# Second layer's combine: three gathered places a tile instead of one running sum

## The chip, the cores and the metric

The kernel runs on one core of one Trainium2 chip. The metric is the device time of one execution in microseconds (us), median of several runs. Engines are called by their names in the profile: PE (TensorE), PEld (its weight loads), DVE (VectorE), ACT (ScalarE), POOL (GpSimd), SP (SyncE, which here only issues DMAs). A queue name such as SPq or POOLq is the part of an engine that issues.

## The reference, cut to what matters

Two layers, each a cross-attention and a mixture-of-experts feed-forward part, work on 2048 tokens of 256 values:

```
x = x + tanh(g_xattn[0]) * L0_xattn(layernorm(x), ctx)
x = x + tanh(g_ffn[0])   * L0_ffn(layernorm(x))      # 8 experts, top 2
x = x + tanh(g_xattn[1]) * L1_xattn(layernorm(x), ctx)
x = x + tanh(g_ffn[1])   * L1_ffn(layernorm(x))      # 16 experts, top 4
return x
# L1_ffn, for the tokens x [2048, 256]:
w_dense = top-4 softmax weights of x @ router_w.T       # [2048, 16]
moe_out = sum over experts e of w_dense[:, e] * (silu(x @ gate_w[e].T) * (x @ up_w[e].T)) @ down_w[e].T
shared  = silu(x @ shared_gate_w.T) * (x @ shared_up_w.T) @ shared_down_w.T
return moe_out + sigmoid(x @ se_gate_w.T) * shared
```

The change is in how the four expert results of a token (moe_out) are brought together in the last line of the kernel's work.

## The kernel before, in words

The 2048 tokens are 16 tiles of 128 (NT = 16), and x_sb holds all of them in on-chip memory (SBUF). In the feed-forward part of the second layer the tokens of each expert are collected into slots of 128 rows. There are 80 such slots in 40 groups (NG[1] = 40), each group with two slots. For a group, POOL gathers token rows (L664), PE multiplies by gate, up and down weights, DVE copies the result to yb (L960), and SP stores it to the table ys[1] in HBM (L649). The tokens' weights are already multiplied in, so a token's expert sum is the plain sum of four rows of ys[1].

The place table says where these four rows are: `place[:, k, t]` holds, for place k of tile t, the row number in ys[1]. Places are in falling order of slot, so place 3 belongs to the lowest expert of a token and place 0 to the highest.

After the last token gather POOL runs `gather_sums(pl, n)` for n = 0 to 3 (L702 to L711). Each n goes over all 16 tiles with place 3 - n. For n = 0 the indirect DMA writes into y_sum[t]; for n = 1 to 3 it adds in memory (`compute_op=ALU.add`). y_sum[t] is one piece of 128x256 f32 a tile, in three old buffers (stg, wqp, xnf). So 16 gathers write and 48 add. Before each n, `needed_rows` (L680) waits until the groups that the n-th expert from the end can reach have been stored; it reads two registers and issues two tiny POOL instructions (L687). From n = 1 on, every second tile waits until the gathers before it on the same two tiles have landed (`sum_ld`, one semaphore for two tiles).

DVE meanwhile works through the shared expert. Its 24 units (NSH = 24: 4 blocks of 512 tokens, 6 units each) are done partly before the expert groups (units 0 to 5) and partly after them, in the loop `for s in range(HALF, NSH + 3)` (L965), where i = s - 6. A step of this loop is: `shared_out` (L884, the block's sum from PSUM into x_sb, four instructions) every sixth step, `shared_product` (L910), `shared_low` of the unit before (L918), and then the combine. PE does gate_up of unit s (L261) and the down product of unit s - 2 (L743), and waits for DVE's products; ACT does the silu (L827) and the high half (L833).

The combine of the second layer starts at step i = 14 (COMBINE_STEP). Steps 14 to 19 take two tiles each, and step 20 the last four. `combine(t)` waits for all four gathers of the tile's pair, then adds y_sum[t] times tga into x_sb[t] (L899), one instruction a tile with a drain ahead of it. SP waits for `c_used` and for the block's shared sum (s_accr), and stores tile t to the output (L658).

The first layer has its own combine (L698 gathers, two places a tile, each written to its own buffer, and two L899 instructions a tile).

## Time and profile before

| what | value |
|---|---|
| time, median of 3 runs | 1030.58 us (1027.38 to 1032.69) |
| the profiled execution | 1020.56 us, of which the span is 1018.8 us |
| PE busy | 826.1 us (81% of the span) |
| DVE busy | 741.0 us (73%) |
| POOL busy | 653.6 us (64%) |
| ACT busy | 475.5 us (47%) |
| granted TensorE clock, mean | 0.836 |

The span is cut into 40 slices of 25.5 us in the profile's second part; the work that changes fills the last four and a half. A row of a timeline gives the start from the span's beginning, the duration, the engine, the source line, the operation, what is written and read, how many instructions of the kind are merged in the row, and in brackets how long the engine was idle before it and what ended that.

### The profile page before, as it was taken

The numbers are of one execution on the slowest core, as the hardware profiler recorded it, in microseconds if no ns is written. First come the engines' busy times: TensorE is split into PE (matmuls) and PEld (weight loads), VectorE is DVE, ScalarE is ACT, GpSimd is POOL, SyncE is SP. The second block draws the span as 40 slices with busy tenths as digits, with TensorE's granted clock in tenths as the row PEclk, the third lists the DMA queues.
The fourth block names the chain that finished last, engine by engine and source line by source line (L and its number), as shares of the span: only waits on it lengthen the run. The fifth ranks groups of instructions, "written<-read, shape, count | busy, mean of one in ns | idle before, by whom it ended". The sixth has DMA issues, their size and how long they took to land.

```text
span 1018.8 us, 20963 instructions
## 1 busy us (share of the span) xinstructions
PE 826.1 (81%) x6776; PEld 560.1 (55%) x6777; DVE 741.0 (73%) x1654; ACT 475.5 (47%) x1078; POOL 653.6 (64%) x834
## 2 busy tenths in 40 slices
PE   4489758789998969888878887876869999999952
PEld 2267544566655536555555554544557777775621
DVE  5778768666757688878987889875858777773424
ACT  3355344233322366777676677753414344342310
POOL 3486973566366777887787787851035444468886
PEclk8689969899999955776686876785979999999977
DMA  7031124245433141221310100002014444455556
GB/s 264 19 87 51 50 86 139 61 149 154 125 101 94 56 144 57 93 70 42 113 28 18 44 13 17 6 2 84 6 45 132 133 140 127 143 153 109 72 79 134
DMA packets 72542, 87.64 MB, mean 86 GB/s; under 512 B 11268, under 2 KB 65288, under 8 KB 72456
## 3 DMA queue, kind: packets, MB, share of 16 engines
q1 hardware_dynamic: 57480, 57.40, 17.5%
q0 software_dynamic: 14976, 29.14, 12.7%
q8 instruction: 48, 0.79, 0.3%
q14 instruction: 38, 0.31, 0.1%
HBM read 64.03 MB, written 32.98 MB: 95 GB/s over the span
## 4 chain that ended last, share of the span: by engine, by line
PE 26%; POOL 16%; DVE 13%; issue 8%; POOLq 4%; DVEq 3%; ACT 2%; DMA 1%; ACTq 0%
PE PS L261 11%; DVE sb_slotv L1389 4%; POOL sb_stg L709 4%; PE PS L804 4%; POOL sb_wqp L709 2%; POOL sb_xnf L709 2%; PE PS L1270 2%; DVE sb_wkh L1394 2%; PE PS L767 2%; PE PS L1260 2%; PE PS L796 1%; PE PS L743 1%; PE PS L398 1%; DVE sb_x_sb L899 1%; DMA sb_xnf<-slot_table,sb_place 1%
## 5 line engine op out<-in xcount | busy, mean ns | idle before, releaser
L664 POOL DMA_INDIRECT sb_xnf<-token_table,sb_ids x120 | 115.9, 966 | 161.9 <-DVE sb_ids L578 74.3
L1389 DVE TENSOR_REDUCE sb_slotv<-PS 128x1 f32<-128x512 f32 x256 | 163.7, 681 | 26.6 <-PE PS L1260 26.6
L261 PE MATMUL PS<-sb_xnT,sb_sgu 128*128 128x512 f16 x528 | 125.0, 389 | 1.1 <-DVE sb_lg L446 0.6
L261 PE MATMUL PS<-sb_region,sb_wkh 128*128 x720 | 121.7, 321 | 4.6 <-issue 2.2
L1344 ACT ACTIVATE sb_wk<-PS,sb_slotv 128x512 f32<-128x512 f32 x128 | 87.0, 690 | 24.5 <-DVE sb_slotv L1389 24.2
L261 PEld LDWEIGHTS PS<-sb_region,sb_wkh 128*128 128x128 f16 x720 | 69.4, 100 | 46.0 <-issue 12.9
L827 ACT ACTIVATE sb_wk<-PS 128x512 f32<-128x512 f32 (+1 forms) x48 | 28.6, 596 | 132.8 <-PE PS L261 120.5
L1728 POOL TENSOR_SCALAR sb_wk<-sb_wk 128x512 f32<-128x512 f32 x128 | 79.3, 620 | 16.6 <-ACT sb_wk L1344 7.1
L743 PE MATMUL PS<-sb_sdn,sb_wkh 128*128 128x256 f16 x544 | 68.5, 276 | 24.9 <-DVE sb_wkh L918 22.5
L261 PEld LDWEIGHTS PS<-sb_xnT,sb_sgu 128*128 128x128 f16 x528 | 52.0, 100 | 58.3 <-issue 6.5
L1394 DVE TENSOR_SCALAR sb_wkh<-PS 128x1024 f16<-128x1024 f16 x112 | 76.6, 684 | 8.5 <-PE PS L1282 8.4
L947 DVE SCALAR_TENSOR_TENSOR sb_wk<-PS,sb_sm,sb_wk 128x176 f32<-128x176 f32 x120 | 42.6, 396 | 51.6 <-ACT sb_wk L855 51.3
L804 PE MATMUL PS<-sb_region,sb_wkh 128*128 x600 | 76.2, 273 | 2.7 <-DVE sb_wa L960 2.3
L743 PEld LDWEIGHTS PS<-sb_sdn,sb_wkh 128*128 128x128 f16 x544 | 52.6, 99 | 44.0 <-DVE sb_wkh L918 28.9
L846 ACT ACTIVATE sb_wkh<-PS 128x512 f16<-128x512 f32 x60 | 35.8, 596 | 81.7 <-PE PS L767 81.7
L910 DVE SCALAR_TENSOR_TENSOR sb_wk<-PS,sb_wk 128x512 f32<-128x512 f32 (+1 forms) x48 | 33.2, 692 | 50.6 <-ACT sb_wk L827 47.4
L855 ACT ACTIVATE sb_wk<-PS 128x352 f32<-128x352 f32 x60 | 27.8, 463 | 90.1 <-PE PS L261 90.1
L804 PEld LDWEIGHTS PS<-sb_region,sb_wkh 128*128 128x128 f16 x600 | 55.8, 97 | 14.3 <-issue 5.8
L1344 ACT ACTIVATE sb_wkh<-PS,sb_slotv 128x512 f32<-128x512 f32 x64 | 43.4, 684 | 33.8 <-DVE sb_slotv L1389 23.1
L1270 PE MATMUL PS<-sb_idh,sb_wk 128*128 128x128 f16 x512 | 53.2, 264 | 1.2 <-POOL sb_wk L1728 0.7
L931 DVE TENSOR_TENSOR sb_wkh<-PS,sb_wkh 128x512 f16<-128x512 f32 x60 | 41.2, 686 | 16.0 <-ACT sb_wkh L846 15.6
L1344 ACT ACTIVATE sb_xnf<-PS,sb_slotv 128x512 f32<-128x512 f32 x64 | 43.4, 685 | 19.4 <-DVE sb_slotv L1389 19.3
(295 smaller groups left out, 1995.3 us busy)
## 6 DMA issues: line engine op xcount, KB each, us to landing
slot_table<-sb_wa SPq DMA_DIRECT2D x60, 256.0 KB, 2.3
slot_table<-token_table SPq DMA_DIRECT2D x16, 640.0 KB
sb_stg<-gu SPq DMA_DIRECT2D x24, 352.0 KB, 3.5
sb_stg<-dn SPq DMA_DIRECT2D x24, 256.0 KB, 2.9
token_table<-sb_xnf SPq DMA_DIRECT2D x16, 256.0 KB, 3.7
sb_stg<-sgu SPq DMA_DIRECT2D x8, 352.0 KB, 5.1
sb_x_sb<-x SPq DMA_DIRECT2D x1, 2048.0 KB, 12.3
out<-sb_x_sb SPq DMA_DIRECT2D x16, 128.0 KB
```

The costliest lines, as they stand in the source:

```text
L261: last = nc.tensor.matmul(out_, lhs(i, c), rhs(j, c), start=(c == 0 and n == 0 and not begun), stop=(c == C - 1 and n == 2 and not more))
L664: nc.gpsimd.indirect_dma_start(xg[l][:, 2 * (g % XR) + n, :], None, xw[l][:, :], bass.IndirectOffsetOnAxis(ap=ids[:, 2 * g + n:2 * g + n + ...
L709: nc.gpsimd.indirect_dma_start(y_sum[t], None, ys[1][:, :], bass.IndirectOffsetOnAxis(ap=place[:, k, t:t + 1], axis=0), compute_op=ALU.add ...
L743: last = nc.tensor.matmul(PS[:, first + i // 2, i % 2 * D:(i % 2 + 1) * D], wkh[:, HR * h + v, i * P:(i + 1) * P], sdn[:, j, k, :], start= ...
L804: last = nc.tensor.matmul(PS[:, 7, n * D:(n + 1) * D], wkh[0:r, 4 + 2 * u + i, (2 * c + n) * P:(2 * c + n + 1) * P], DN[l][0:r, bass.ds(e[ ...
L931: nc.vector.tensor_tensor(wkh[:, 2 * (s % 2) + 1, :], PS[:, 4 + s % 2, :], wkh[:, 2 * (s % 2), :], ALU.subtract).then_inc(e_xl[l].sem, 1)
L947: last = nc.vector.scalar_tensor_tensor(wk1[:, 2 + u, n * EI:(n + 1) * EI], PS[:, 2 * u + n, EI:EG], wv[u][:, n:n + 1], wk1[:, u, n * EI:( ...
L1270: last = nc.tensor.transpose(bank[:, (h * KT + k) * P:(h * KT + k + 1) * P], h_p[s % NE][:, h, k * P:(k + 1) * P], idh[:, :])
L1344: nc.scalar.activation(h_e[s % NE][:, h, :], PS[:, 2 * u + h, :], ACT.Exp, bias=h_nb[u][:, h:h + 1], accum_out=o_sum[v][:, head:head + 1]) ...
L1389: nc.vector.tensor_reduce(h_nb[u][:, h:h + 1], PS[:, 2 * u + h, :], AX, ALU.max, negate=True).then_inc(h_max, 1)
L1394: nc.vector.tensor_scalar(h_T[s % 2], PS[:, 4 + s % 2, :].bitcast(F16), -RB, None, ALU.add).then_inc(h_pc_dve, 1)
L1728: nc.gpsimd.tensor_scalar(h_e[s % NE][:, h], h_e[s % NE][:, h], 255.0, MAGIC + RB_BITS, ALU.mult, ALU.add).then_inc(h_int, 1)
```

## The change

The four gathers of a tile no longer all go into one buffer. Place 3 is written to y_sum[t] and place 2 is added to it in memory, as before. Place 1 is written to a new buffer y_high[t], and place 0 to a new buffer y_last[t]. Both lie in `region`, where the expert weights of the second layer were. So 48 gathers write and 16 add. The order on POOL is written out in `combine_rows`: 6 writes of place 3; then 10 times an add of place 2 and a write of place 3; then 6 times an add of place 2 and a write of place 1; then 10 writes of place 1; then 16 writes of place 0. `needed_rows` stands ahead of these parts as before (0, 1, 2, 3).

DVE adds three buffers a tile into x_sb instead of one, 48 instructions instead of 16: `combine_low` for two tiles a step from step i = 6 on (8 steps), `combine_high` for two tiles a step from i = 14 to 19 and for the last four at i = 20, and `combine_last` for all 16 tiles at i = 20. Each of these begins with one drain, with none between its tiles. c_used, which releases the output stores, is now raised only by `combine_last`.

The first layer's combine does the same as before in fewer branches.

```diff
--- before.py
+++ after.py
@@ -251,7 +251,7 @@
             nc.vector.tensor_scalar(ve[:, first:end], mv[:, first:end, 1], LN_EPS, None, ALU.add).then_inc(stats_ready, 1)
 
         EARLY = LATE = 4
-        COMBINE_STEP = 14
+        LOW_STEP, HIGH_STEP = 6, 14
         STATS_STEPS = (4, 8, 14)
 
         def mm3(out_, lhs, rhs, more=False, begun=False):
@@ -328,6 +328,7 @@
         e_st = list(zip(*(both(f"e_st{u}", 16 * len(range(u, NG[0], 2))) for u in range(2))))
         c_ld, sum_ld = (list(w) for w in zip(*(both(f"c_ld{r}", 16 * TOPK[0] * NT // CR) for r in range(CR))))
         sum_ld += [Count(sem(f"sum_ld{r}"), 0) for r in range(CR, NT // 2)]
+        high_ld = [Count(s.sem, s.start + 32 * len(range(u, NG[1], XR))) for u, s in enumerate(e_ld[1])]
         c_used = both("c_used", NT)
 
         xnf_flat = xnf[:, :, :].rearrange("p t d -> p (t d)")
@@ -344,6 +345,8 @@
         yr = [xnf_flat[:, r * 2 * D:(r + 1) * 2 * D].rearrange("p (k d) -> p k d", d=D) for r in range(CR)]
         y_sum = [w[:, n * D:(n + 1) * D] for w, tiles in ((stg_flat, 8), (wqp32, 4), (xnf_flat[:, 12 * D:16 * D], 4))
                  for n in range(tiles)]
+        y_high = [reg32[:, t * D:(t + 1) * D] for t in range(NT)]
+        y_last = [reg32[:, (NT + t) * D:(NT + t + 1) * D] for t in range(NT)]
         past_ready = sem("past_ready")
         table_zeroed = sem("table_zeroed")
         wv = [sm[:, 12 + u, 0:2] for u in range(2)]
@@ -699,16 +702,49 @@
                                              bass.IndirectOffsetOnAxis(ap=place[:, k, t:t + 1], axis=0))\
                     .then_inc(c_ld[r].sem, 16)
 
-        def gather_sums(pl, n):
-
-            k = TOPK[1] - 1 - n
-            needed_rows(pl, n)
-            for t in range(NT):
-                if n > 0 and t % 2 == 0:
-                    at_least(pl, sum_ld[t // 2], 0, 32 * n)
-                nc.gpsimd.indirect_dma_start(y_sum[t], None, ys[1][:, :],
-                                             bass.IndirectOffsetOnAxis(ap=place[:, k, t:t + 1], axis=0),
-                                             compute_op=ALU.add if n > 0 else ALU.bypass).then_inc(sum_ld[t // 2].sem, 16)
+        def gather_tile(pl, place_, k, t, done, add=False):
+
+            nc.gpsimd.indirect_dma_start(place_[t], None, ys[1][:, :],
+                                         bass.IndirectOffsetOnAxis(ap=place[:, k, t:t + 1], axis=0),
+                                         compute_op=ALU.add if add else ALU.bypass).then_inc(done.sem, 16)
+
+        ROWS_AHEAD = 6
+        OWN_LAST = range(0, NT)
+
+        def write_low(pl, t):
+            gather_tile(pl, y_sum, 3, t, sum_ld[t // 2])
+
+        def add_low(pl, t):
+            if t % 2 == 0:
+                at_least(pl, sum_ld[t // 2], 0, 32)
+            gather_tile(pl, y_sum, 2, t, sum_ld[t // 2], add=True)
+
+        def write_high(pl, t):
+            gather_tile(pl, y_high, 1, t, high_ld[t // 4])
+
+        def write_last(pl, t):
+            if t % 2 == 0:
+                at_least(pl, sum_ld[t // 2], 0, 64)
+            gather_tile(pl, y_last, 0, t, sum_ld[t // 2])
+
+        def combine_rows(pl):
+
+            needed_rows(pl, 0)
+            for t in range(ROWS_AHEAD):
+                write_low(pl, t)
+            needed_rows(pl, 1)
+            for t in range(ROWS_AHEAD, NT):
+                add_low(pl, t - ROWS_AHEAD)
+                write_low(pl, t)
+            needed_rows(pl, 2)
+            for t in range(ROWS_AHEAD):
+                add_low(pl, NT - ROWS_AHEAD + t)
+                write_high(pl, t)
+            for t in range(ROWS_AHEAD, NT):
+                write_high(pl, t)
+            needed_rows(pl, 3)
+            for t in OWN_LAST:
+                write_last(pl, t)
 
         def shared_sums(l, s):
 
@@ -887,18 +923,41 @@
 
             def combine(t):
 
-                if l == 0:
-                    r = t % CR
-                    at_least(dve, c_ld[r], 0, 16 * TOPK[0] * (t // CR + 1))
-                    parts = [yr[r][:, k, :] for k in range(TOPK[0])]
-                else:
-                    at_least(dve, sum_ld[t // 2], 0, 32 * TOPK[1])
-                    parts = [y_sum[t]]
-                for y in parts:
+                r = t % CR
+                at_least(dve, c_ld[r], 0, 16 * TOPK[0] * (t // CR + 1))
+                for k in range(2):
                     dve.drain()
-                    last = nc.vector.scalar_tensor_tensor(x_sb[:, t, :], y, tga[:, l:l + 1],
+                    last = nc.vector.scalar_tensor_tensor(x_sb[:, t, :], yr[r][:, k, :], tga[:, 0:1],
                                                           x_sb[:, t, :], ALU.mult, ALU.add)
-                last.then_inc(c_used[l].sem, 1)
+                last.then_inc(c_used[0].sem, 1)
+
+            def add_rows(t, y):
+
+                return nc.vector.scalar_tensor_tensor(x_sb[:, t, :], y[t], tga[:, 1:2], x_sb[:, t, :], ALU.mult, ALU.add)
+
+            def combine_low(*tiles):
+
+                dve.drain()
+                for t in tiles:
+                    at_least(dve, sum_ld[t // 2], 0, 64)
+                    add_rows(t, y_sum)
+
+            def combine_high(*tiles):
+
+                dve.drain()
+                for t in tiles:
+                    of_four = range(t // 4 * 4, t // 4 * 4 + 4)
+                    at_least(dve, high_ld[t // 4], 0, 16 * (4 + sum(1 for i in of_four if i not in OWN_LAST)))
+                    last = add_rows(t, y_high)
+                    if t not in OWN_LAST:
+                        last.then_inc(c_used[1].sem, 1)
+
+            def combine_last(*tiles):
+
+                dve.drain()
+                for t in tiles:
+                    at_least(dve, sum_ld[t // 2], 0, 96)
+                    add_rows(t, y_last).then_inc(c_used[1].sem, 1)
 
             def shared_product(s):
                 u, k = s % 2, s % KSH
@@ -974,9 +1033,13 @@
                     shared_low(s - 1)
                 if l == 0 and 1 <= i < 1 + NT - LATE:
                     combine(i - 1)
-                if l == 1 and i >= COMBINE_STEP:
-                    for t in range(2 * (i - COMBINE_STEP), 2 * (i - COMBINE_STEP) + 2 if s < NSH + 2 else NT):
-                        combine(t)
+                if l == 1 and 0 <= i - LOW_STEP < NT // 2:
+                    combine_low(2 * (i - LOW_STEP), 2 * (i - LOW_STEP) + 1)
+                if l == 1 and i >= HIGH_STEP and s < NSH + 2:
+                    combine_high(2 * (i - HIGH_STEP), 2 * (i - HIGH_STEP) + 1)
+                if l == 1 and s == NSH + 2:
+                    combine_high(*range(2 * (i - HIGH_STEP), NT))
+                    combine_last(*OWN_LAST)
                 if l == 0 and i in STATS_STEPS:
                     b = STATS_STEPS.index(i)
                     stats(*range(4 * b, 4 * b + 4))
@@ -1810,8 +1873,7 @@
             attn1_pool(pl, inverse_deviation)
             inverse_deviation(4)
             ffn_pool(pl, 1)
-            for n in range(TOPK[1]):
-                gather_sums(pl, n)
+            combine_rows(pl)
 
         @block.scalar
         def _(act):
```

## Rows read from the trace of the kernel before

**Rows 1.** The chain that ended last, its shares by engine and by line.
```profile
PE 26%; POOL 16%; DVE 13%; issue 8%; POOLq 4%; DVEq 3%; ACT 2%; DMA 1%; ACTq 0%
PE PS L261 11%; DVE sb_slotv L1389 4%; POOL sb_stg L709 4%; PE PS L804 4%; POOL sb_wqp L709 2%; POOL sb_xnf L709 2%; PE PS L1270 2%; DVE sb_wkh L1394 2%; PE PS L767 2%; PE PS L1260 2%; PE PS L796 1%; PE PS L743 1%; PE PS L398 1%; DVE sb_x_sb L899 1%; DMA sb_xnf<-slot_table,sb_place 1%
```

**Rows 2.** Timeline of POOL, the second layer's row gathers (L709).
```profile
903.04 0.96 POOL L709 DMA_INDIRECT sb_stg<-slot_table,sb_place  x1
...
921.82 0.95 POOL L709 DMA_INDIRECT sb_xnf<-slot_table,sb_place  x1 [0.30 <-issue]
922.78 0.33 POOL L687 TENSOR_TENSOR sb_past_seen<-sb_mhalf 1x1 f32<-1x1 f32 x2
923.26 1.61 POOL L709 DMA_INDIRECT sb_stg<-slot_table,sb_place  x1
...
981.49 1.56 POOL L709 DMA_INDIRECT sb_xnf<-slot_table,sb_place  x1 [0.30 <-issue]
982.48 0.69 POOL L687 TENSOR_TENSOR sb_past_seen<-sb_mhalf 1x1 f32<-1x1 f32 x2
983.39 1.56 POOL L709 DMA_INDIRECT sb_stg<-slot_table,sb_place  x1 [0.23 <-issue]
...
1011.20 1.55 POOL L709 DMA_INDIRECT sb_xnf<-slot_table,sb_place  x1 [0.30 <-issue]
```

**Rows 3.** The chain in order of time: start, us, what; last pieces.
```profile
1011.20 4.32 DMA sb_xnf<-slot_table,sb_place
...
1016.19 0.49 DVE sb_x_sb L899
```

**Rows 4.** The first layer's row gathers: line L698, and its group with mean.
```profile
L698 POOL DMA_INDIRECT sb_xnf<-slot_table,sb_place x32: 942/946/1312, 283.8 to 345.3; - x32
...
DMA to landing us min/median/max: 2.7/2.8/5.6
...
L698 POOL DMA_INDIRECT sb_xnf<-slot_table,sb_place x32 | 31.1, 971 | 27.1 <-DMA slot_table<-sb_wa 15.7 <-issue 8.0 <-DVE sb_x_sb L899 3.2
```

**Rows 5.** Timeline of PE, shared expert of the second layer.
```profile
946.98 2.75 PE L261 MATMUL PS<-sb_xnT,sb_sgu 128*128 128x512 f16 x12
...
958.68 1.46 PE L261 MATMUL PS<-sb_xnT,sb_sgu 128*128 128x512 f16 x6
...
968.65 2.75 PE L261 MATMUL PS<-sb_xnT,sb_sgu 128*128 128x512 f16 x12
...
976.45 2.75 PE L261 MATMUL PS<-sb_xnT,sb_sgu 128*128 128x512 f16 x12
...
1002.79 1.05 PE L743 MATMUL PS<-sb_sdn,sb_wkh 128*128 128x256 f16 x8 [1.83 <-DVE sb_wkh L918]
```

**Rows 6.** Timeline of DVE in the same stretch.
```profile
948.33 1.66 DVE L884 SCALAR_TENSOR_TENSOR sb_x_sb<-PS,sb_sgate,sb_x_sb 128x256 f32<-128x256 f32 x4
...
960.80 0.69 DVE L910 SCALAR_TENSOR_TENSOR sb_wk<-PS,sb_wk 64x512 f32<-64x512 f32 x1 [1.31 <-ACT sb_wk L827]
961.41 0.68 DVE L918 TENSOR_TENSOR sb_wkh<-sb_wk,sb_wkh 128x512 f16<-128x512 f32 x1
...
989.10 1.06 DVE L899 SCALAR_TENSOR_TENSOR sb_x_sb<-sb_stg,sb_tga,sb_x_sb 128x256 f32<-128x256 f32 x2 [15.74 <-DMA sb_stg<-slot_table,sb_place]
```

**Rows 7.** Output stores, line L658: duration ns min/median/max, first and last start.
```profile
L658 SPq DMA_DIRECT2D out<-sb_x_sb x16: 332/332/877, 989.6 to 1016.7; - x16
```

**Rows 8.** DMA queues in 903:923, 928:950, 985:1010: packets, MB, share of 16 engines.
```profile
q0 software_dynamic: 740, 2.05, 37.6%
...
q0 software_dynamic: 1665, 1.51, 48.6%
...
q1 hardware_dynamic: 1452, 1.32, 16.8%
```

**Rows 9.** A gather that starts beside a DVE instruction with two SBUF inputs.
```profile
943.99 1.87 POOL L709 DMA_INDIRECT sb_wqp<-slot_table,sb_place  x1 [0.30 <-issue]
...
943.76 0.69 DVE L918 TENSOR_TENSOR sb_wkh<-sb_wk,sb_wkh 64x512 f16<-64x512 f32 x1
```

## The prediction, on record before the changed kernel was run

> **What bounds the kernel now.** I read the chain of waits first. Its shares by line show the second layer's row gathers, L709, on POOL with 8% in three groups, and POOL with 16% in all [rows 1]. The timeline of POOL then shows where they lie: without a break from 903.04 to the end, 64 of them, the last issued at 1011.20 [rows 2]. That one lands 4.32 us later, at 1015.52, DVE adds its two tiles until 1016.68 [rows 3], the last output store is issued at 1016.7 [rows 7], and the span ends at 1018.8, 2.1 us after it. So from 903 on the stream of gathers sets the end. DVE and PE wait for it: DVE stood idle for 15.74 us until 989.10 [rows 6], and PE, whose last unbroken work ends at 979.2 (976.45 + 2.75), did its last product at 1002.79 [rows 5].
>
> In that stream there are two prices. The 16 writes start 1.252 us apart ((921.82 - 903.04) / 15), with 0.95 us each as duration. The 48 adds start 1.854 us apart ((1011.20 - 983.39) / 15) and last 1.55 [rows 2]. An add therefore costs 0.60 us more on POOL. The first add also falls near the end of the expert work, so the price could belong to the stretch and not to the operation. The first layer's gathers speak against that: they run beside the same shared-expert work, all write, and have a median of 0.946 us [rows 4].
>
> **The change part by part.**
>
> *The gathers.* 64 stay 64; 32 of the 48 adds become writes. From 903.04 to the start of the last one there are 47 writes and 16 adds: 47 x 1.252 + 16 x 1.854 = 58.8 + 29.7 = 88.5 us. Three `needed_rows` cost about 0.1 us each, since 921.82 to 923.26 is 1.44 where 1.25 is usual, and 981.49 to 983.39 is 1.90 where 1.85 is usual [rows 2]: 0.3 us. Sum: the last gather starts at 991.8, 19.4 us earlier.
>
> *Gathers held by DVE.* Some gathers start while DVE runs an instruction with two SBUF inputs, and are longer: 1.87 instead of 1.55 [rows 9]. The change has 48 such DVE instructions instead of 16. In the first layer, where 32 gathers run beside 25 of them, the mean is 0.971 against a median of 0.946, which is 0.8 us in all, and the longest is 1.31 [rows 4]. I take 1.0 us more than before; bounds 0 and 5.8 (16 pairs of adds, each meeting one gather, 0.36 us each, from 1.31 - 0.95). The last gather then starts at 992.8.
>
> The Trainium skill, "SBUF — State Buffer", § Who interferes with whom, says that a VectorE instruction with two SBUF inputs contends with a GpSimd instruction that reads SBUF, and that whoever came second waits for the other's end. By that rule alone the added instructions speak against the change. Rows 4 and 9 agree that it happens, and price it at a fraction of a microsecond a meeting.
>
> *Landing.* A write lands 2.8 us after its start [rows 4], an add 4.32 [rows 3]. The last write lands at 995.6; bounds 2.7 and 5.6 [rows 4], so 995.5 to 998.4.
>
> *Waits moved.* `needed_rows(1)` is asked at 910.7 instead of 922.8. All token gathers precede 903.04 in POOL's order, and the last of them waits for 36 of the 40 groups, so the groups up to expert 13 (60 of the 71 slots filled, counted by the reference's routing on its inputs) are long stored. Behind it would stand every later gather; I cost it at 0. An add waits for the writes of its pair, issued 6 tiles, or 18 us, earlier: 0. Adds start 3.1 us apart from 910.8; the tenth lands at 943, the sixteenth, issued at 957.4, at 961.7.
>
> *DVE in the steps.* `combine_low` adds two instructions (0.4 to 0.58 us each, about 1 us) to steps 6 to 13, which begin at 943 to 968.6. DVE is idle 1.31 us or more ahead of the product in such steps [rows 6], so PE loses nothing. The tightest wait is that of the last pair: landed at 961.7, asked at 970. If this cover were gone, the worst is 1 us a step in 8 steps, but PE and ACT would have to stand on it, which the idle time excludes. `combine_high` in steps 14 to 19 asks for writes that landed by 974.6 at the latest. The 15.74 us wait goes.
>
> *What is late next.* The shared expert now runs through. One block of six units takes 968.65 - 946.98 = 21.67 us on PE [rows 5]. The last unit's product on DVE has its like at 960.80 [rows 6], so it comes at 982.5. Then: end of product 983.2, low part of the unit before and two `combine_high` instructions to 984.8, low part 0.68 to 985.5, the down product 1.05 [rows 5] to 986.5, while DVE does two more pairs of `combine_high` until 987.5, `shared_out` 1.66 [rows 6] with its wait to 989.3, and four `combine_high` to 991.0. Only now comes `combine_last` with all 16 tiles. Four instructions of this size without a drain between them take 1.66 us [rows 6], 0.40 apart; two with a drain take 1.06, 0.58 apart. The new ones have no drain but each has a semaphore to raise and some a wait; I take 0.45: 16 x 0.45 + 0.1 = 7.3 us, end at 998.3 (bounds 997.5 and 1000.4). The last two gathers landed at 995.6, so DVE no longer waits for POOL: the end passes from POOL to PE and DVE.
>
> *Output.* Before, twelve of the 16 output stores left while gathers ran. Now all 16 leave after 991. Issuing costs SP 0.33 us each [rows 7], under DVE's 0.45. Data: of the 16 DMA engines' time a store of 0.131 MB takes 0.168 x 25 x 0.131 / 1.32 = 0.42 us, a written gather 0.376 x 20 x 0.131 / 2.05 = 0.48, an added one 0.486 x 22 x 0.131 / 1.51 = 0.93 [rows 8]. Sixteen stores and the last four gathers ask 6.7 + 1.9 = 8.6 us from 991.3, that is until 999.9, and the store's own 2.1 us contain some 1.7 of latency: 1001.6. By DVE alone it is 998.3 + 0.05 + 2.1 = 1000.5. I take 1001.5; bounds 999.7 and 1004.
>
> **Sum.** Span 1001.5 instead of 1018.8: 17.3 us less. The profiled execution took 1020.56, so it becomes 1003.3. The median of the runs shown is 10.0 us above it. The stretch changed is the same in both, so I carry the difference over: 1030.58 - 17.3 = 1013.3 us.
>
> **Rivals.**
>
> *A. The tail is dearer.* DVE's last adds stand 0.58 apart, or the stores and gathers queue: 991.0 + 9.4 = 1000.4, and two or three microseconds of queueing behind full DMA engines give 1004.5 to 1005. Gain 14, 1016.6 us. For it: the burst asks as much as the engines have. Against: 0.40 apart in L884.
>
> *B. DVE's two-input adds hold the gathers* by the 5.8 us of the bound: last start 997.6, landing 1000.4, DVE to 1001.4, end 1003.5 plus 0.7 for the stores. Gain 14.6, 1016 us. This is what the skill's rule above would make of it at its strongest; the mean of rows 4 is against.
>
> *C. A write issued among adds costs as much as an add,* because the queue behind POOL is slowed by adds still in it (an add asks 0.93 us of the DMA engines). The 16 writes that alternate with adds cost 0.60 more, 9.6 us: last start 1002.4, landing 1005.2, DVE 1006.1, end 1008.2. Gain 10.6, 1020.0 us. No row shows a write behind an add.
>
> *D. Slower: once an add has been issued, every later gather is slow.* Place: POOL, from the first add on. Then 6 writes are cheap and 58 gathers dear: 903.04 + 6 x 1.252 + 57 x 1.854 + 0.3 = 1016.5; landing 2.8 to 4.3 later, 1019.3 to 1020.8; 0.9 for DVE and 2.1 for the store: 1022.3 to 1023.8. It decides against the change when more than about 34 of the 42 later writes stay dear: 32 of them make up the 48 dear gathers of before, and a write that lands 1.5 us sooner than an add pays for two more. With all 42: 1030.58 + 4.3 = 1034.9 us. For it: the L687 pair takes 0.33 ahead of the first add and 0.69 after [rows 2]. Against: the pair at 982.48 starts 0.99 us after the gather's start, as at 922.78 (0.96), and then lasts until that gather ends, so POOL's sequencer works at the old pace and only the add itself has a tail of 0.6.
>
> **Chances.** Forecast 0.62, A 0.16, B 0.05, C 0.10, D 0.05, something else 0.02. Under 0.5% (5 us) is what a measurement of this kernel can't tell from no change; forecast, A, B and C are all beyond it. D lies at it and is split; with the spread of the runs I give faster 0.91, same 0.05, slower 0.04. The likeliest case's bounds, gains of 19.1 and 14.8, give 1011.5 to 1015.8, and the runs before lie 3.2 below to 2.1 above their median. With C included the range is 1008 to 1021.
>
> **What would show it.** On POOL: 1.25 us between writes after adds too, the last gather near 992 to 993 (C: 1002; D: 1016). On DVE: no wait in steps 6 to 19, `combine_last` beginning at 991, at 0.4 to 0.58 us a tile; the last store near 998.5. PE: no gap at 979, last product near 986. The prediction is wrong if a gather that writes lasts over 1.1 us beside adds, if DVE waits for a gather in `combine_last`, or if the stores end over 4 us after DVE.

## The result, and the profile after

The changed kernel took 1043.86 us (median of 4 runs, 1041.64 to 1046.83), beside 1028.98 for the kernel before (4 runs, 1025.53 to 1032.69): ratio 1.0146, 95% interval 1.0100 to 1.0192. Forecast were 1013.3 us and a gain. It became slower, by about as much as it was to become faster.

| us | before | changed, first result | changed, last set |
|---|---|---|---|
| median, and the kernel before beside it | 1028.98 | 1043.86 (1028.98) | 1007.25 (1022.98) |
| profiled execution, its span | 1020.56, 1018.8 | 1041.64, 1039.9 | 1003.68, 1001.9 |
| first, last of the 64 gathers starts | 903.04, 1011.20 | 910.05, 1002.00 | 901.67, 994.50 |
| PE's last product ends | 1003.8 | 1025.1 | 985.3 |
| DVE's last add ends | 1016.7 | 1035.9 | 999.7 |

The third column is the last experiment: the same program, in another set of runs, came out close to the forecast. First the slower one.

POOL's timeline of the changed kernel, the columns as in [rows 2], answers to those rows:

```profile
910.05 0.96 POOL L707 DMA_INDIRECT sb_stg<-slot_table,sb_place  x1
...
917.78 1.61 POOL L707 DMA_INDIRECT sb_stg<-slot_table,sb_place  x1
919.70 1.00 POOL L707 DMA_INDIRECT sb_stg<-slot_table,sb_place  x1 [0.31 <-issue]
921.00 1.54 POOL L707 DMA_INDIRECT sb_stg<-slot_table,sb_place  x1 [0.30 <-issue]
...
982.70 0.33 POOL L690 TENSOR_TENSOR sb_past_seen<-sb_mhalf 1x1 f32<-1x1 f32 x2
...
1002.00 0.95 POOL L707 DMA_INDIRECT sb_region<-slot_table,sb_place  x1 [0.30 <-issue]
```

The stream takes 91.95 us from first start to last instead of 108.16. A write between two adds lasts 0.97 to 1.02, an add mostly 1.54 or 1.55, and the L690 pair at 982.70, with only writes before it, is back to 0.33. So POOL did its part. But the end has left POOL. The chain of waits from 985 on (start, us, what):

```profile
986.85 15.92 issue
...
1004.24 1.89 PE PS L779 x8
...
1019.10 1.31 PE PS L261 x6
...
1031.99 3.96 DVE sb_x_sb L936 x10
```

No gather stands in it, where [rows 3] had one. For 15.92 us the engine on the chain waited for nothing that the profile shows. The timelines of ACT and then PE say which:

```profile
983.87 0.59 ACT L863 ACTIVATE sb_wk<-PS 64x512 f32<-64x512 f32 x1 [5.32 <-PE PS L261]
...
1002.14 0.60 ACT L863 ACTIVATE sb_wk<-PS 128x512 f32<-128x512 f32 x1 [17.16 <-issue]
```

```profile
980.99 2.75 PE L261 MATMUL PS<-sb_xnT,sb_sgu 128*128 128x512 f16 x12
985.84 1.48 PE L779 MATMUL PS<-sb_sdn,sb_wkh 128*128 128x256 f16 x12 [2.10 <-issue]
...
990.23 1.07 PE L261 MATMUL PS<-sb_xnT,sb_sgu 128*128 128x512 f16 x3 [1.01 <-issue]
992.33 1.09 PE L261 MATMUL PS<-sb_xnT,sb_sgu 128*128 128x512 f16 x3 [1.02 <-issue]
1004.24 1.89 PE L779 MATMUL PS<-sb_sdn,sb_wkh 128*128 128x256 f16 x8 [10.82 <-DVE sb_wkh L977]
```

PE does three matmuls in the 2.1 us that it needs for nine (12 take 2.75). Then it has done what it can without DVE's next product. ACT stands 17.16 us and goes on at 1002.14, 0.14 us after POOL has started its last gather. After that the old pace returns (twelve L261 take 3.65 at once behind the stall, then 2.75 again), and DVE's end is the forecast one:

```profile
1002.77 0.69 DVE L969 SCALAR_TENSOR_TENSOR sb_wk<-PS,sb_wk 128x512 f32<-128x512 f32 x1 [16.02 <-issue]
...
1026.02 1.66 DVE L920 SCALAR_TENSOR_TENSOR sb_x_sb<-PS,sb_sgate,sb_x_sb 128x256 f32<-128x256 f32 x4
1027.77 8.18 DVE L936 SCALAR_TENSOR_TENSOR sb_x_sb<-sb_region,sb_tga,sb_x_sb 128x256 f32<-128x256 f32 x20
```

The 20 adds (four `combine_high`, 16 `combine_last`) take 8.18 us, 0.40 apart. The stores (L661 here) answer to [rows 7]; the last is issued 1.8 us after DVE's last add, and the span ends 2.2 us later:

```profile
L661 SPq DMA_DIRECT2D out<-sb_x_sb x16: 332/399/411, 1030.0 to 1037.7; - x16
...
DMA to landing us min/median/max: 1.7/1.8/2.0
```

The DMA queues in 980 to 1003 (packets, MB, share of 16 engines), the view of [rows 8]:

```profile
q0 software_dynamic: 857, 2.36, 35.6%
q8 instruction: 1, 0.02, 0.3%
```

The 16 DMA engines are thus not full: the gathers take a third of their time, less than the 48.6% that adds take in the kernel before [rows 8] while PE is fully busy. There is an earlier, smaller stall at 916 to 924 (ACT 7.24 and 4.45 us, DVE 3.51 and 3.87). Both are called stalls here: an engine stands or crawls, and the chain or the timeline names `issue`, or `remote`, a releaser that the profile can't name.

### The profile page after: what moved, and what is told of

It is laid out like the page before. It is cut to its first block and busy times, and to the rows that moved or that the text cites. A ratio compares the mean times of both kernels' runs of the same rounds, so it can differ in the third digit from the quotient of the medians.

```text
span 1039.9 us, 20995 instructions
## 1 busy us (share of the span) xinstructions
PE 833.9 (80%) x6776; PEld 564.2 (54%) x6777; DVE 752.5 (72%) x1686; ACT 476.3 (46%) x1078; POOL 640.0 (62%) x834
## 3 DMA queue, kind: packets, MB, share of 16 engines
q1 hardware_dynamic: 57480, 57.40, 17.3%
## 5 line engine op out<-in xcount | busy, mean ns | idle before, releaser
L261 PE MATMUL PS<-sb_xnT,sb_sgu 128*128 128x512 f16 x528 | 126.5, 390 | 3.9 <-issue 3.1
L261 PE MATMUL PS<-sb_region,sb_wkh 128*128 x720 | 122.5, 321 | 4.9 <-issue 3.8
L261 PEld LDWEIGHTS PS<-sb_region,sb_wkh 128*128 128x128 f16 x720 | 69.6, 100 | 46.3 <-issue 13.4
L1791 POOL TENSOR_SCALAR sb_wk<-sb_wk 128x512 f32<-128x512 f32 x128 | 79.8, 623 | 15.7 <-ACT sb_wk L1407 6.2
L261 PEld LDWEIGHTS PS<-sb_xnT,sb_sgu 128*128 128x128 f16 x528 | 52.2, 100 | 62.9 <-issue 12.7
L840 PE MATMUL PS<-sb_region,sb_wkh 128*128 x600 | 78.0, 277 | 6.8 <-issue 3.7
L803 PE MATMUL PS<-sb_idf,sb_xnf 128*128 128x128 f32 x240 | 39.0, 287 | 18.1 <-DMA sb_xnf<-token_table,sb_ids 17.8
```

Source lines behind the costliest of these rows:

```text
L261: last = nc.tensor.matmul(out_, lhs(i, c), rhs(j, c), start=(c == 0 and n == 0 and not begun), stop=(c == C - 1 and n == 2 and not more))
L803: last = nc.tensor.transpose(PS[:, 4 + s % 2, (2 * n + c) * P:(2 * n + c + 1) * P], xg[l][:, 2 * (s % XR) + n, c * P:(c + 1) * P], idf[:, :])
L840: last = nc.tensor.matmul(PS[:, 7, n * D:(n + 1) * D], wkh[0:r, 4 + 2 * u + i, (2 * c + n) * P:(2 * c + n + 1) * P], DN[l][0:r, bass.ds(e[ ...
L1791: nc.gpsimd.tensor_scalar(h_e[s % NE][:, h], h_e[s % NE][:, h], 255.0, MAGIC + RB_BITS, ALU.mult, ALU.add).then_inc(h_int, 1)
```

## The experiments

The question was why ACT, PE and DVE stand with nothing to wait for. Theories: the writes of POOL, closely spaced, starve them; DVE's 32 added instructions with two SBUF inputs do it; the length or the shape of the instruction stream does it; or it is something that differs from one set of runs to the next, such as the chip. A set is the runs that were made together on one chip, each with the kernel before among them. What each run was expected to show stands as it was put on record.

### Four variants in one set (kernel before beside them: 1022.82; chip 6)

*e1*: the kernel before, but all 64 gathers write, so the sum of a row's four places is left out.

```diff
-    compute_op=ALU.add if n > 0 else ALU.bypass)
+    compute_op=ALU.bypass)
```

> The kernel before, with its 48 adding gathers turned into writes of the same rows to the same places (the sums are left out). POOL then issues 64 written gathers in the old order; DVE and the rest are as before. Theory D (dense writes: a gather every 1.25 us from POOL keeps ACT, DVE and PE from going on, as in the changed kernel's profile, where ACT stood still for 17 us until POOL's last gather): stalls of several us on ACT or PE between 903 and 985, and an end no earlier than about 1005. Theory M (it is the alternation of adding and writing gathers that does it): no stalls, last gather at 903 + 63 x 1.25 = 982, end near 995, a gain of 20 to 25 us. Theory L (the added DVE instructions moved the places at which the instruction streams are reloaded): no stalls either, same number as M.

Measured 997.26, ratio 0.9764 (0.9726 to 0.9802), first gather 901.8, last 982.8.

*e2*: the changed kernel in its order, but places 1 and 0 are added onto what lay in their buffers, so the sums are not those of the reference.

```diff
-            gather_tile(pl, y_high, 1, t, high_ld[t // 4])
+            gather_tile(pl, y_high, 1, t, high_ld[t // 4], add=True)
...
-            gather_tile(pl, y_last, 0, t, sum_ld[t // 2])
+            gather_tile(pl, y_last, 0, t, sum_ld[t // 2], add=True)
```

> The changed kernel, with the gathers of places 1 and 0 adding into their new buffers instead of writing (the sums come out with what lay there before; 48 adds, 16 writes). Same order, same DVE work, same program length. Theory D: adds are 1.85 us apart, so the stalls of ACT and PE after 950 vanish, the stream ends at about 1018 and the kernel at about 1022 to 1026 of a profile, no slower than the changed kernel. Theory L or a theory of the destination (writes into the weights' buffer): stalls stay, end beyond 1040.

Measured 1023.99, ratio 1.0022 (0.9997 to 1.0047).

*e3*: the changed kernel with four one-element instructions on POOL behind each write.

```diff
+            for i in range(0 if add else 4):
+                at = next(pauses)
+                nc.gpsimd.tensor_tensor(pause[:, at:at + 1], mhalf[0:1, 0:1], mhalf[0:1, 0:1], ALU.add)
```

> The changed kernel, with four one-element POOL instructions (0.17 us each by the L687 pair) behind every written gather, so that writes too are about 1.9 us apart. All else as in the changed kernel. Theory D: stalls vanish; the stream takes 64 x 1.85 = 118 us from its start, end near 1025 of a profile. Theory L and the destination theory: stalls of several us stay, and the end is beyond 1040.

Measured 1033.19, ratio 1.0102 (1.0071 to 1.0133). The last 16 writes then start 2.0 us apart, the last one at 1034.5 (in the profiled execution, which at 1043.91 was the slowest of five). The pause costs more than the change can bring.

*e4*: the changed kernel without `combine_low` and `combine_high`, so places 1 to 3 are left out.

```diff
-                if l == 1 and 0 <= i - LOW_STEP < NT // 2:
-                    combine_low(2 * (i - LOW_STEP), 2 * (i - LOW_STEP) + 1)
-                if l == 1 and i >= HIGH_STEP and s < NSH + 2:
-                    combine_high(2 * (i - HIGH_STEP), 2 * (i - HIGH_STEP) + 1)
...
-                    combine_high(*range(2 * (i - HIGH_STEP), NT))
```

> The changed kernel without combine_low and combine_high (places 1 to 3 are left out of x); POOL's stream as in the changed kernel, DVE has 32 instructions with two SBUF inputs fewer. Theory D: ACT and PE stall all the same, end about 1038, 2 us less than the changed kernel. A theory that the added DVE instructions hold POOL or the instruction streams: stalls vanish, end near 1000.

Measured 1006.83, ratio 0.9858 (0.9820 to 0.9895).

None of the four shows the stall: e1, with 64 writes and no pause, has PE busy 20.00 of 20 us in 925:945. e4 seemed to say that DVE's added instructions are the cause. It was read too soon, since the changed kernel itself was not in the set.

### Are DVE's added instructions the cause? (kernel before: 1029.68; chip 15)

The next set had the changed kernel, and three variants of DVE's work: *e5* does `combine_low` and `combine_high` only after the last `shared_out`; *e6* adds 4 of the 256 columns in both, which leaves out the others; *e7* leaves out `combine_low`, and with it places 3 and 2.

```diff
 (e5)
-                    combine_high(*range(2 * (i - HIGH_STEP), NT))
+                    combine_low(*range(NT))
+                    combine_high(*range(NT))
 (e6)
-                    add_rows(t, y_sum)
+                    add_rows(t, y_sum, 4)
...
-                    last = add_rows(t, y_high)
+                    last = add_rows(t, y_high, 4)
 (e7)
-                if l == 1 and 0 <= i - LOW_STEP < NT // 2:
-                    combine_low(2 * (i - LOW_STEP), 2 * (i - LOW_STEP) + 1)
```

> The changed kernel once more, unchanged, beside the kernel before. It asks whether the time of 1044 us and the stalls of ACT and PE between 911 and 1002 are the program's own or came once. Theory L (the program's streams of instructions and the gathers meet always at the same places): the same 1040 to 1047 us, with stalls at the same steps. Theory S (they meet by chance): another time, or stalls at other steps; under 1010 us where there are none.

> The changed kernel with all 48 adds of DVE behind the last shared_out; none is left in the steps beside the gathers. The result is the same and DVE's program as long as the changed one's. Theory P (DVE's adds with two SBUF inputs beside densely written gathers cause the stalls): none is left, the end is that of e4_no_low_high plus 32 x 0.40 = 13 us, about 1020 us. Theory L: stalls depend on where the instructions lie, and may stay: over 1030.

> The changed kernel with combine_low and combine_high adding 4 of a tile's 256 columns (the rest of places 1 to 3 is left out). Same instructions, waits, drains and places, but each holds SBUF for about 0.07 us instead of 0.48. Theory P: stalls vanish or shrink, about 1007 us as e4_no_low_high. Theory W (the instructions' number, waits and drains, or their place in the stream, cause it): stalls stay, about 1040.

> The changed kernel without combine_low (places 3 and 2 are left out); combine_high stays in steps 14 to 20. Stalls in the changed kernel's profile began while combine_low ran (steps 6 to 12). Theory P: fewer meetings, a time between 1007 (e4_no_low_high) and 1040, nearer to the first since combine_high meets only the last dozen gathers. Theory L: either of the two.

Measured: changed 1046.49, ratio 1.0164 (1.0116 to 1.0213); e5 1056.26, 1.0272 (1.0217 to 1.0326); e6 1042.64, 1.0148 (1.0091 to 1.0205); e7 1044.42, 1.0136 (1.0083 to 1.0189). All stall. In e5 DVE has none of the added instructions before 1031.10, and yet ACT stands twice; PE's timeline shows the crawl at its clearest:

```profile
996.31 0.59 PE L261 MATMUL PS<-sb_xnT,sb_sgu 128*128 128x512 f16 x1 [1.72 <-issue]
998.41 0.59 PE L261 MATMUL PS<-sb_xnT,sb_sgu 128*128 128x512 f16 x1 [1.51 <-issue]
999.82 0.58 PE L261 MATMUL PS<-sb_xnT,sb_sgu 128*128 128x512 f16 x1 [0.83 <-issue]
1001.21 1.71 PE L261 MATMUL PS<-sb_xnT,sb_sgu 128*128 128x512 f16 x3 [0.81 <-issue]
```

```profile
985.85 0.60 ACT L863 ACTIVATE sb_wk<-PS 128x512 f32<-128x512 f32 x1 [12.38 <-remote]
1002.03 0.59 ACT L863 ACTIVATE sb_wk<-PS 64x512 f32<-64x512 f32 x1 [15.07 <-remote]
```

Single matmuls start 1.4 or 2.1 us apart, and the crawl ends about 4 to 5 us after the last gather's start (996.9). In the changed kernel of this set ACT stands 25.57 us, until 1003.41; in e6 15.84, in e7 15.85. Neither the place, nor the size, nor the number of DVE's added instructions takes the stall away. That theory fell.

### Is it the length of the stream? (kernel before: 1030.17; chip 0)

*e8* is the kernel before with 40 more instructions at DVE's end; *e9* the changed kernel with DVE adding four tiles in one instruction (two in `combine_last`), which makes DVE's stream shorter than that of the kernel before; *e10* is e9 with the 40.

```diff
 (e8, e10)
+            for _ in range(40):
+                dve.drain()
 (e9, e10)
-                if l == 1 and 0 <= i - LOW_STEP < NT // 2:
-                    combine_low(2 * (i - LOW_STEP), 2 * (i - LOW_STEP) + 1)
...
+                if l == 1 and i in LOW_STEPS:
+                    combine_low(*range(4 * LOW_STEPS.index(i), 4 * LOW_STEPS.index(i) + 4))
```

 The changed kernel has 2333, e5_adds_at_end 2320, e7_no_low 2309, e6_small_adds 2333, and all four (and the changed kernel again) stalled at the same places, also in the first layer's gathers, which the change doesn't touch; the kernel before and e1_all_write have 2301 and e4_no_low_high 2286, and did not. Theory N (over 2304 DVE instructions, the engines stall while POOL gathers): 15 to 30 us slower than the kernel before, with the stalls of ACT near 911 and 300. Theory K (the kernels of the first set ran on a chip that doesn't stall, those of the second on one that does; the program's length is nothing): within 3 us of the kernel before.

> The changed kernel's order of gathers and its result, with DVE adding four tiles an instruction for low (steps 7, 9, 10, 13) and high (steps 15, 16, 18, 19) and two for last: 16 adds instead of 48, and 2298 DVE instructions. Theory N: no stalls, last gather 92 us after the first, end near 1000 of a profile, 15 to 20 us under the kernel before. Theory K: on a stalling chip as slow as the changed kernel, about 1040.

> e9_short_four_tiles with 40 more DVE drains behind the last DVE instruction: 2338 DVE instructions, all that is done while gathers run is as in e9. Theory N: 25 to 40 us slower than e9, near the changed kernel. Theory K: within 3 us of e9.

> The changed kernel on the same chip as these. Theory N: about 1.5% slower than the kernel before, as in both earlier looks. Theory K: it tells which kind of chip this is: 1.5% slower on one that stalls, about 1.5% faster, with the 17 us of the forecast, on one that doesn't.

Measured: e8 1029.03, ratio 0.9997 (0.9975 to 1.0019); e9 1050.12, 1.0176 (1.0133 to 1.0219); e10 1047.73, 1.0170 (1.0131 to 1.0209); changed 1054.51, 1.0198 (1.0147 to 1.0249). The length does nothing, neither way. But e8, which is the kernel before in all but its end, was the find. Its timelines of PE and ACT:

```profile
922.10 0.45 PE L261 MATMUL PS<-sb_region,sb_wkh 128*128 x1 [1.65 <-issue]
923.51 0.45 PE L261 MATMUL PS<-sb_region,sb_wkh 128*128 x1 [0.96 <-issue]
925.60 0.45 PE L261 MATMUL PS<-sb_region,sb_wkh 128*128 x1 [1.64 <-issue]
...
940.73 2.31 PE L804 MATMUL PS<-sb_region,sb_wkh 128*128 x10 [1.81 <-issue]
942.83 2.30 PE L261 MATMUL PS<-sb_region,sb_wkh 128*128 x12
...
951.84 7.93 PE L261 MATMUL PS<-sb_xnT,sb_sgu 128*128 128x512 f16 x36 [0.26 <-issue]
```

```profile
933.34 0.46 ACT L855 ACTIVATE sb_wk<-PS 128x352 f32<-128x352 f32 x1 [19.13 <-PE PS L261]
```

The kernel before stalls too, here: from about 911 on, while its 16 writes are issued (starts 907.62 to 926.39), and on beside the first seven of its adds (from 927.83), until 940.73. The other 41 adds run without a stall. Busy time in stretches of 20 us (columns: PE, its weight loads, DVE, ACT, POOL, granted clock, DMA share, GB/s), first e8, then the profile of before that the prediction had read:

```profile
905.00:925.00 20.00, 11.08 (x66) 7.37 (x64) 5.10 (x13) 2.01 (x5) 15.39 (x18) 0.78 0.43 127
925.00:945.00 20.00, 7.65 (x32) 4.03 (x32) 5.37 (x13) 2.69 (x7) 16.65 (x14) 0.54 0.49 85
...
965.00:985.00 20.00, 20.00 (x122) 11.77 (x121) 8.82 (x16) 5.57 (x10) 16.66 (x11) 1.00 0.49 69
```

```profile
905.00:925.00 20.00, 18.06 (x127) 12.16 (x125) 11.52 (x27) 5.27 (x14) 15.43 (x18) 1.00 0.61 183
925.00:945.00 20.00, 20.00 (x124) 11.93 (x122) 7.83 (x12) 6.67 (x12) 16.77 (x11) 1.00 0.49 70
```

Against the second, PE is busy 6.98 + 12.35 = 19.3 us less in these 40 us, and what it does is slower, at a granted clock of 0.54 in the second window: ten L804 take 2.31 us where they took 1.26 (910.38 in the profile of before). The shared expert's first matmuls show the whole delay. They stand above at 951.84, which is 44.2 us behind the first gather (907.62); in the profile of before it is 17.1 us (903.04):

```profile
920.14 7.93 PE L261 MATMUL PS<-sb_xnT,sb_sgu 128*128 128x512 f16 x36 [0.25 <-issue]
```

So PE is 27.1 us late. Most of that is hidden, since DVE would have waited for the gathers anyway ([rows 6]: 15.74 us and more behind it). But it is no longer the gathers that set the end. DVE's last rows in e8 show no wait for a gather, where those of [rows 3] hang on the last one:

```profile
1017.44 2.21 DVE L899 SCALAR_TENSOR_TENSOR sb_x_sb<-sb_wqp,sb_tga,sb_x_sb 128x256 f32<-128x256 f32 x4
...
1021.50 2.21 DVE L899 SCALAR_TENSOR_TENSOR sb_x_sb<-sb_xnf,sb_tga,sb_x_sb 128x256 f32<-128x256 f32 x4
```

The chain of waits from 1000 on runs through PE, ACT and DVE, with no gather in it. The last gather starts at 1016.44 and by the 4.32 us of [rows 3] lands near 1020.8 (an estimate), 0.7 us before DVE comes to it. The span ends 9.5 us after the last gather's start, against 7.6 in the profile of before: so in this profile the kernel before is held by PE and DVE, and gathers that end 16 us sooner could win back 1.9 us at most.

The stalls also mark a place that the change doesn't touch. The first layer's 32 row gathers, all writes, spread over 66.5 us in e8, and over 61.5 in [rows 4]:

```profile
L698 POOL DMA_INDIRECT sb_xnf<-slot_table,sb_place x32: 940/946/1460, 285.1 to 351.6; - x32
```

In all nine profiles with stalls at the end of the kernel this stretch is 64.9 to 66.8 us long, in the eleven without 61.1 to 63.4. ACT stands in it for 5.76 and 5.32 us with releaser `remote` in e8, and never so in the profile of before.

### The first set again (kernel before: 1024.70; chip 15)

> e1_all_write again (the kernel before, 64 written gathers, the sums left out). Its first look was beside a kernel before at 1022.8 us; in the other sets, where that is 1029 to 1030, e8_before_longer shows PE at one matmul in 0.7 to 2.1 us while the 16 written gathers run and for 4 us of the adds behind them, and back at its pace then. Theory D (on such a chip densely written gathers starve PE, ACT and DVE of instructions, adding gathers don't): stalls of 20 us and more within 903 to 985, end near 1030 instead of 993. Theory K2 (chip alone, the kind of gather is nothing): PE stalls here no more than in e8.

> e2_high_last_add again (the changed kernel, places 1 and 0 added into their buffers): the adds begin as in the changed kernel, but there are only 16 writes, each beside adds. Theory D: a stall near 911 to 925 as in the changed kernel, none from 950 on; end near 1026, set by POOL, 15 to 20 us under the changed kernel's 1044 to 1054. Theory K2: stalls after 975 as in the changed kernel, end over 1040.

> e3_paced_writes again (the changed kernel, four tiny POOL instructions behind each written gather, gathers about 1.9 us apart). Theory D by the gap between writes: no stall over 5 us after 950, end near 1035, set by POOL. Theory D by the kind of gather alone (what a written gather puts into the queue, whatever the gap): stalls stay, end over 1045.

> e4_no_low_high again (the changed kernel without the adds of low and high). Theory D: as slow as the changed kernel less 2 us, 1040 to 1050, with the same stalls of ACT after 975: DVE's added instructions have nothing to do with them, and the 1006.8 us of its first look was the chip's. Theory P (DVE's adds cause the stalls): 1005 to 1012 again.

Measured: e1 998.40, ratio 0.9739 (0.9691 to 0.9788); e2 1024.66, 1.0004 (0.9981 to 1.0028); e3 1035.31, 1.0097 (1.0062 to 1.0132); e4 1006.52, 0.9814 (0.9765 to 0.9862). The ratios of the first set repeat, again without a stall, and again with a kernel before that takes under 1025. So two explanations were left: these four kernels, by their form, do not stall, or these two sets were made where nothing stalls.

### The changed kernel and all writes, side by side (kernel before: 1022.98; chip 9)

> The changed kernel once more. Theory K, that it is the chip (or the machine it stands in) which decides: where the kernel before takes about 1023 to 1025 us beside it, the changed kernel shows no stall of PE, ACT and DVE among its written gathers and takes 1003 to 1010 us; where the kernel before takes about 1029 to 1031 us, it takes 1042 to 1055 us as in the three sets with it so far, with ACT and DVE standing for 15 us or more at the end of the gathers. Theory F, that it is the form of this kernel (where its instructions lie) and not the chip: 1042 us or more with the stalls, whatever the kernel before takes.

> The kernel before with all 64 gathers of the second combine written, which leaves its sums out. Theory D, that a dense stream of written gathers starves the other engines where the chip is of the slower kind: if the kernel before takes 1029 to 1031 us beside it, PE, ACT and DVE stand or crawl during the 80 us of writes, and it ends near or above 1015 us; on the other kind it takes 997 to 1000 us, 0.974 of the kernel before, as in both sets so far. Theory F, the form of the changed kernel: this kernel takes 997 to 1004 us and shows no stall on either kind of chip.

Measured: the changed kernel 1007.25 (1003.68 to 1013.75), ratio 0.9866 (0.9815 to 0.9918); e1 996.45, ratio 0.9731 (0.9689 to 0.9774). The same program that had lost 1.5 to 2.0% three times now gains 1.3%. So it isn't the kernel's form: something that differs between sets decides. That it is the chip is not shown. The set with e5 to e7, in which all four kernels stalled, ran on chip 15, and so did, 39 minutes later, the one with e1b to e4b, in which none did. Either one chip does both, or the number doesn't name one chip alone. Windows of 20 us of the changed kernel in this set, the last one that in which the shared expert ends, and then in the first result, where the last one is that of the stall:

```profile
905.00:925.00 20.00, 17.95 (x123) 11.74 (x122) 10.35 (x24) 5.81 (x15) 15.97 (x16) 1.00 0.67 166
945.00:965.00 20.00, 20.00 (x128) 12.31 (x126) 13.96 (x27) 6.68 (x12) 16.04 (x14) 1.00 0.42 87
965.00:985.00 20.00, 19.12 (x125) 11.97 (x124) 14.77 (x29) 6.20 (x11) 15.87 (x17) 1.00 0.34 98
```

```profile
905.00:925.00 20.00, 15.42 (x92) 10.37 (x90) 7.16 (x20) 4.20 (x11) 14.57 (x18) 0.78 0.48 129
945.00:965.00 20.00, 20.00 (x124) 11.97 (x123) 8.57 (x14) 6.69 (x12) 16.49 (x15) 1.00 0.42 80
985.00:1005.00 20.00, 5.74 (x28) 2.83 (x29) 3.77 (x8) 1.11 (x2) 13.68 (x15) 0.74 0.36 103
```

Without stalls the tail is the forecast one, but for its last two pieces. The timelines of PE, DVE and POOL:

```profile
984.24 1.05 PE L779 MATMUL PS<-sb_sdn,sb_wkh 128*128 128x256 f16 x8 [0.18 <-DVE sb_wkh L977]
```

```profile
987.98 6.59 DVE L936 SCALAR_TENSOR_TENSOR sb_x_sb<-sb_region,sb_tga,sb_x_sb 128x256 f32<-128x256 f32 x16
996.14 0.88 DVE L936 SCALAR_TENSOR_TENSOR sb_x_sb<-sb_region,sb_tga,sb_x_sb 128x256 f32<-128x256 f32 x2 [1.57 <-DMA sb_region<-slot_table,sb_place]
998.81 0.88 DVE L936 SCALAR_TENSOR_TENSOR sb_x_sb<-sb_region,sb_tga,sb_x_sb 128x256 f32<-128x256 f32 x2 [1.79 <-DMA sb_region<-slot_table,sb_place]
```

```profile
992.99 1.21 POOL L707 DMA_INDIRECT sb_region<-slot_table,sb_place  x1 [0.30 <-issue]
994.50 0.95 POOL L707 DMA_INDIRECT sb_region<-slot_table,sb_place  x1 [0.30 <-issue]
```

e1 beside it doesn't test the writes where kernels stall, since none of its three sets was such a one.

## Why the prediction was wrong, by its own steps

**The step that failed** is the first one, "So from 903 on the stream of gathers sets the end", together with the carrying over at the sum: "The stretch changed is the same in both, so I carry the difference over". Both were read from one profile without stalls. The runs shown were, by their times, made with stalls, and there e8 shows the kernel before held by PE and DVE, with 1.9 us to win instead of 17.3. A sign was in the numbers: the profiled execution, at 1020.56, lay 6.8 us under the fastest of the three runs (1027.38). The prediction noted a distance of 10.0 us and took it for an offset; it was a difference in what happens in the stretch. The kernel before takes 1022.8 to 1024.7 in the three sets without stalls and 1029.0 to 1030.2 in the three with them.

**What is late next** failed with it where kernels stall. "The shared expert now runs through", last product at 986.5: it ended at 1025.1. Against the run without stalls that is 39.8 us later, of which 8.4 are the later start of the gathers (910.05 against 901.67; 4.8 of them arise in the first layer's gathers, which took 66.3 us instead of 61.5) and 31.4 the stalls with the slower clock behind them. "PE and ACT would have to stand on it, which the idle time excludes" looked only at DVE's added work; they stood for another reason.

Why is the changed kernel slower, and not merely no faster? Against e8, the profiled span is 14.0 us longer (1039.9 against 1025.9). Of these, 2.4 are the start of the gathers (910.05 against 907.62) and 4.2 a longer way from there to PE's last product (115.1 against 110.8 us). The largest part, 7.3, is the way from that product to the end (14.8 against 7.4 us), with 20 adds on DVE behind `shared_out` where the kernel before has four. In the set beside e8 the changed kernel has the same 14.7 us of tail, and 126.9 from the first gather to the last product. So the change moves the stall rather than removing it (12.7 us behind the first writes instead of 27.1, then a second one beside the 26 writes at the end), and it puts DVE's adds on the way that now sets the end. e5, with all 48 of them there, is 9.8 us slower still than the changed kernel beside it.

**The gathers** were right: 1.25 us a write, 1.85 an add. From first start to last 88.8 us were forecast without DVE's holding, 91.95 and 92.8 measured. **Gathers held by DVE**, taken at 1.0, were thus 3 to 4 us in these two profiles, within the bound of 5.8 (1.7 and 2.2 in two more, where DVE stood longer). e4, without DVE's added instructions in the steps, still has 92.1 and 91.1, so at most about 1.7 of it comes from those; a gather is held by the instructions that were there before as well. Some 0.5 us of it is not holding at all, but the 16 writes beside adds at 0.98 instead of 0.95.

**Landing**: 4.28 us for the last write, in the chain of waits of the run without stalls, not 2.8. It falls among the 16 stores, whose median landing was 1.8 us in the first result, with the gathers over, and 2.9 here; that the one delays the other is likely, but no run separates them. The bound 5.6 held it.

**DVE in the steps** costs nothing where nothing stalls: the changed kernel's 1007.25 against 1006.83 and 1006.52 without these adds, though in different sets. **Waits moved** cost nothing: no gather waited on `needed_rows`.

**The tail**: the last product at 985.3, forecast 985.1 when moved by the 1.4 us by which the gathers start earlier; the 16 adds 0.40 apart, not 0.45. Then DVE waits 1.57 and 1.79 us for the last gathers and ends at 999.7 instead of 998.3 - 1.4 = 996.9: the end did not pass from POOL to PE and DVE, it stayed with POOL. The span is 1001.9, forecast 1001.5, and the gain by medians is 15.7 us, forecast 17.3. That the span comes so close is partly luck: the last gather started 3.1 us later than forecast (994.5 against 992.8 - 1.4) and landed 1.5 us more slowly; against that stand a stream that began 1.4 us earlier and stores that ended 2.2 us after DVE, where 3.2 had been allowed.

**The rivals.** A: 0.58 us a tile was wrong (0.40); queueing at the end is there, but is in the landing of gathers. B: the holding came to 3 to 4 us of its 5.8. C: a write behind an add lasts 0.97 to 1.02, not 1.55 (but for one in each profile, 1.21 and 1.50, the latter beside two DVE instructions with two SBUF inputs). D: after the last add writes are back at 0.95. It had the right sign for the wrong reason; none of the four had other engines that stand while POOL gathers. Of the prediction's own signs of being wrong, "if DVE waits for a gather in `combine_last`" came true even where the time was as forecast.

**What stays open.** That written gathers bring the stalls on rests on their place in time. All nine profiles with stalls have the first layer's 32 writes drawn out, and a stall near the start of the second layer's stream (its 16 writes in e8; six writes from 910.05 in the changed kernel), and the eight of the changed kernel and its variants again near its plain writes at the end (from 968.15 in the first result); ACT's last stalled wait ends there 0.1 to 5.1 us after the last gather's start. The fit is loose: in e8 the stall outlasts the start of the last write by 14 us and goes on beside seven adds, and in the first result PE keeps its pace for 15 us of plain writes before it slows at 983.7. An all-write kernel and an all-add kernel for comparison (e1, and e2 with 48 adds) never fell in a set with stalls, and neither did the paced writes of e3, so writes, their spacing and the chance of the place are not told apart there. What the engines lack is argued, not shown: "issue" says that they wait for nothing recorded, single instructions come at a steady 0.7, 1.4 or 2.1 us, and it would fit a late supply of instructions. The Trainium skill, "Runtime: NRT & Kernel Launch", § Instruction fetch mechanics, says that an engine's instruction memory is refilled in blocks of 16 KiB through a DMA queue of its sequencer, and that this is mostly hidden. The trace has such packets (0.02 MB each on q8), so few that they show no lateness by themselves. The Trainium skill, "SBUF — State Buffer", § Who interferes with whom, also says that PE and ACT never wait on anyone; of SBUF's ports that may hold, but here ACT stood up to 25.78 us (e10) while POOL issued DMAs. What makes one set stall and another not was not found.

## What to carry to other kernels

Compare the profiled execution with the runs before using its spans: one that lies 6.8 us under the fastest run may show a course of events that the runs don't have, and the stretch to be changed must then be seen in both. A stretch that the change leaves alone can tell them apart, as the first layer's gathers do here (61 to 63 us against 65 to 67). Slack is cover for whatever goes wrong beneath it, and it may be used up already; before a change relies on 16 us of it, run the kernel before more than once and look at what its last waits are. Work that is moved behind the last wait costs its full time once that wait is gone: 20 adds, 8.2 us. And when variants are compared, the changed kernel itself belongs in every set: the first set left it out, and until the next a difference between sets passed for an effect of DVE's adds.

## What of the hardware was not expected

- In three of six sets ACT, DVE and PE stand for up to 26 us, or PE issues a matmul every 0.7 to 2.1 us instead of every 0.23 (2.75 / 12), in stretches in which POOL issues indirect DMAs that write and for up to 14 us after them; the 16 DMA engines are 36 to 49% busy in the windows shown above. Kernel before: 1029.0 to 1030.2 us in these sets, 1022.8 to 1024.7 in the others; changed kernel: 1043.9 to 1054.5 in these, 1007.25 in one of the others. Chip 15 was in a set of either kind.
- An indirect DMA with add costs POOL 1.54 us and a written one 0.95, and 0.97 to 1.02 when it stands between adds; the price goes with the operation and hardly with what stands beside it.
